# Attention in unrolled half-groups: row maxima from row-tiled pairs, probabilities summed over key tiles on VectorE and GpSimd, and a short product with ones

## What is computed

```python
q, k, v = (n(x) @ Wq), (n(x) @ Wk), (n(x) @ Wv)       # n = layernorm; 16 heads, 2 x 16 wide
q, k = rotary(q), rotary(k)
for w in (0, 1):                                       # each head has two query/key pairs
    s_w = q_w @ k_w.T * scale ; masked causally
    attn_w = softmax(s_w) @ v                          # the same v (32 wide) for both
attn = lowpass_over_time(attn_1 - lambda * attn_2)     # FFT, filter, inverse FFT
attn = rms_normalise(attn, 32 wide) ; out = x + attn @ Wout
```

## Time and profile before

| | us |
|---|---|
| median of three runs | 1475.98 (1471.82 to 1480.4) |
| the profiled execution | 1487.37 |
| its span, first to last instruction | 1485.3 |
| `attention`: first projection to first `rows` matmul | 78.89 to 134.98 |
| `attention`: groups in steady order, to the last copy of `acc` | 166.98 to 1025.6 |
| PE busy, of the span | 82% |
| ACT busy, of the span | 55% |
| DVE busy, of the span | 55% |
| POOL busy, of the span | 36% |
| mean granted clock of TensorE (1.0 is full) | 0.902 |

### The profile page before, as it was taken

One profiled execution on the slowest core, in us unless ns is written; L12 is line 12 of the kernel. 1 busy time (PEld: TensorE's weight loads), 2 busy tenths in 40 slices (PEclk: granted clock), 3 DMA queues, 4 the chain that ended last, 5 costly groups with the idle time before them and its releaser, 6 DMA issues. The chain is left out here.

```text
span 1485.3 us, 20587 instructions
## 1 busy us (share of the span) xinstructions
PE 1224.6 (82%) x6617; PEld 636.3 (43%) x6632; DVE 814.1 (55%) x1518; ACT 821.2 (55%) x1757; POOL 529.8 (36%) x487
## 2 busy tenths in 40 slices
PE   5954789789789889789789788788479999996996
PEld 4722233333333333333333332423257777774453
DVE  5644553563663663563563563731756666653775
ACT  2303587787787787687787789775312222220221
POOL 4434404226226226225326321020015656563111
PEclk9986669999989989889989989979879999998997
DMA  4356530620620630620530620300421121102331
GB/s 140 117 135 103 84 55 22 104 34 36 110 29 36 100 38 37 104 36 35 86 54 36 94 31 15 116 2 15 155 80 57 65 71 68 47 32 98 119 107 42
DMA packets 68972, 102.04 MB, mean 69 GB/s; under 512 B 8065, under 2 KB 34305, under 8 KB 68865
## 3 DMA queue, kind: packets, MB, share of 16 engines
q1 hardware_dynamic: 58368, 71.34, 24.3%
q0 software_dynamic: 5888, 20.97, 3.7%
q10 hardware_dynamic: 4608, 8.39, 1.5%
HBM read 66.74 MB, written 33.95 MB: 68 GB/s over the span
## 5 line engine op out<-in xcount | busy, mean ns | idle before, releaser
L1056 ACT ACTIVATE score<-score,nmax 128x1024 f32<-128x1024 f32 (+7 forms) x512 | 364.8, 713 | 167.0 <-DVE nmax L932 83.0
L1086 ACT ACTIVATE prob<-score 128x1024 f32<-128x1024 f32 (+3 forms) x384 | 298.2, 812 | 46.4 <-PE score L793 29.3
L774 PE MATMUL score<-kst,qst 96*128 96x512 bf16 (+3 forms) x768 | 219.8, 366 | 96.5 <-ACT score L1056 76.0
L935 DVE TENSOR_REDUCE nmax<-score 128x1 f32<-128x640 f32 (+3 forms) x256 | 251.0, 1019 | 86.7 <-PE score L778 82.6
L789 PE MATMUL score<-qst,kst 99*128 99x512 bf16 (+3 forms) x768 | 221.8, 359 | 25.1 <-ACT score L1056 9.7
L932 DVE TENSOR_REDUCE nmax<-score 128x2 f32<-128x256 f32 (+3 forms) x128 | 105.2, 824 | 243.2 <-PE score L778 243.2
L718 PE MATMUL misc<-xnT,wg 128*128 128x512 f32 x256 | 139.7, 645 | 24.3 <-DVE raw L872 16.7
L774 PEld LDWEIGHTS score<-kst,qst 96*128 96x128 bf16 x768 | 63.4, 103 | 223.6 <-ACT score L1056 147.0
L789 PEld LDWEIGHTS score<-qst,kst 99*128 99x128 bf16 x768 | 75.1, 104 | 195.7 <-ACT prob L1086 70.8
L778 PE MATMUL score<-mask_s,identb 128*128 128x128 bf16 x512 | 115.8, 236 | 0.0
L793 PE MATMUL score<-mask_t,identb 128*128 128x128 bf16 x512 | 111.3, 240 | 0.0
(11 more groups left out here) (219 smaller groups left out, 2054.1 us busy)
## 6 DMA issues: line engine op xcount, KB each, us to landing
piece_scratch<-pieces POOLq DMA_DIRECT2D x16, 768.0 KB, 4.1
qst<-piece_scratch SPq DMA_DIRECT2D x48, 256.0 KB, 9.5
kst<-piece_scratch SPq DMA_DIRECT2D x48, 256.0 KB, 18.4
x1in<-in_query SPq DMA_DIRECT2D x16, 256.0 KB, 2.7
v_scratch<-v ACTq DMA_DIRECT2D x16, 256.0 KB, 2.0
vg<-v_scratch SPq DMA_DIRECT2D x8, 512.0 KB, 15.0
att_scratch<-y SPq DMA_DIRECT2D x8, 512.0 KB, 2.7
m_aT<-att_scratch SPq DMA_DIRECT2D x16, 256.0 KB, 2.9
```

The costliest lines, as they stand in the source:

```text
L774: mm = nc.tensor.matmul(score[slot][:, bank, 0:w], qst[0:PIECES, g.slot, pair + k, i * P:(i + 1) * P], kst[0:PIECES, g.slot, pair + k, c0: ...
L935: nc.vector.tensor_reduce(nmax[:, pair, i:i + 1], src[:].rearrange("p a b -> p (a b)")[:, 0:(i + 1) * P], AX.X, ALU.max, negate=True).then ...
L1056: ins = nc.scalar.activation(s, s, ACT.Exp, bias=nmax[:, pair + k, i:i + 1], accum_out=den[:, pair + k, i:i + 1])
L1086: nc.scalar.activation(prob[:, u % NPROB, :, t0:HALF], score[slot][:, :, t0:HALF], ACT.Exp).then_inc(s_exp, 1)
```

## The change

- **Half-groups.** A group is worked on as two sets, one for each query/key pair number, of four heads. There are 16 sets; all of them are written out, there is no loop. Stacks `qst` and `kst` have three slots of four heads.
- **`rows` units give the maximum only.** They use the coarse half of the stack: three products of pieces, 48 rows. Even heads keep those rows at partitions 0 to 47, odd heads at 64 to 111 (`BANDS`, `COARSE`), and the matmuls of an even and an odd head are issued one after the other into two banks. A unit is at most 512 columns wide. There is no exp and no sum on ACT; the bank is free when DVE has taken the maximum. Masks of two heads are added by one matmul.
- **`probs` units** are one head each, in one bank, with the full stack (depth 98 or 112). They subtract the negated maximum alone (two bf16 rows), so the probabilities are not normalised.
- **PSUM**: five banks in a ring (`RING`), two for `acc`, one for `misc`.
- **Sums of probabilities**: a tile holds one key tile for four heads. Tiles 0, 4 and 8 of 12 are bases; the tiles 1, 2, 3, 9, 10 and 11 are added to them by DVE and 5, 6 and 7 by POOL, in fp32. `denominators` multiplies the three bases with a matrix of ones, 32 columns a head, into `misc`; ACT forms 1/sum by Ln and Exp (`norm`).
- **`output`** multiplies `acc` with 1/sum, and for the second set with -lambda too (DVE); `vn` and `scale_v` go.
- **Evacuations**: ACT copies out projections, turns and low pass, which DVE did before.
- **DMAs**: 24 for a set's stacks instead of 12 for a group; the same bytes, each DMA a quarter of the size. The shift rows go by one DMA out and two in, for each half of a set.
- All `rows` units of a set are done ahead, merged pair by pair with the 24 pairs of `probs` units of the set before.

The diff, cut to its core:

```diff
 def rows_units():
     units = []
     for i in range(TB):
-        n = 2 if (i + 1) * P <= HALF else 1
-        units += [(i, a, n) for a in range(0, NP, n)]
+        for c0 in range(0, (i + 1) * P, HALF):
+            width = min(HALF, (i + 1) * P - c0)
+            n = 2 if width <= HALF // 2 else 1
+            for first in range(0, 2, n):
+                for odd in range(2):
+                    units.append((i, c0, width, [2 * x + odd for x in range(first, first + n)]))
     return units
...
+BANDS = ((0, 16, 32, 48, 64, 80), (64, 80, 96, 16, 32, 48))
+COARSE = (slice(0, 3 * D), slice(64, 64 + 3 * D))
+VALUES_LATER, ADD_LATER, DEN_LATER, OUT_LATER, SWAP_LATER, SUMS_LATER, MISC_FREE = 3, 4, 7, 10, 4, 6, 3
+BASES = {0: "dve", 4: "pool", 8: "dve"}
+def schedule():
+    pairs += [("rows", 0, u) for u in range(0, NRU, 2)]
+    for n in range(SETS):
+        mine = [("probs", n, m) for m in range(0, NPU, 2)]
+        ahead = [("rows", n + 1, u) for u in range(0, NRU, 2)] if n + 1 < SETS else []
+        pairs += merge(mine, ahead)
...
-        score = [ctx.enter_context(nc.psum_tensor(f"score{i}", [P, 2, HALF], F32)) for i in range(NSLOT)]
-        acc = ctx.enter_context(nc.psum_tensor("acc", [P, HALF], F32))
+        score = [ctx.enter_context(nc.psum_tensor(f"score{i}", [P, HALF], F32)) for i in range(RING)]
+        acc = [ctx.enter_context(nc.psum_tensor(f"acc{i}", [P, HALF], F32)) for i in range(2)]
...
+            def slot_free(k):
+                if k >= RING:
+                    kind, count = done[k - RING]
+                    pe.wait_ge(s_max if kind == "rows" else s_exp, count)
+            def rows(n, u):
+                for x in range(len(heads)):
+                    for odd in range(2):
+                        c, head = COARSE[odd], RU[u + odd][3][x]
+                        mm = nc.tensor.matmul(banks[odd][:, x], qst[c, n % SLOTS, head, i * P:(i + 1) * P],
+                                              kst[c, n % SLOTS, head, c0:c0 + width], start=(x == 0),
+                                              stop=(x == len(heads) - 1), skip_group_check=True)
+                if diag:
+                    for odd in range(2):
+                        nc.tensor.matmul(banks[odd][:, :, width - P:width], identb[:], mask, start=False, stop=True,
+                                         skip_group_check=True).then_inc(s_unit, 1)
+            def denominators(n, h):
+                for b in bases:
+                    for head in range(GH):
+                        mm = nc.tensor.matmul(misc[head * 2 * D:(head + 1) * 2 * D], ones[:], tile_of(n, b)[:, head],
+                                              start=(b == bases[0]), stop=(b == bases[-1]), skip_group_check=True)
...
-                    ins = nc.scalar.activation(s, s, ACT.Exp, bias=nmax[:, pair + k, i:i + 1],
-                                               accum_out=den[:, pair + k, i:i + 1])
+            def add(n, v):                       # on DVE; the same on POOL
+                total = tile_of(n, b)[:, :, t0:HALF]
+                nc.vector.tensor_tensor(total, total, tile_of(n, v)[:, :, t0:HALF], ALU.add).then_inc(s_add["dve"], 1)
+            def norm(n, h):
+                nc.scalar.activation(rden[:, q % 2], misc[:], ACT.Ln).then_inc(s_mread, 1)
+                nc.scalar.activation(rden[:, q % 2], rden[:, q % 2], ACT.Exp, scale=-1.0).then_inc(s_rden, 1)
...
+            for n in range(SETS):                # SP
+                if n + 2 < SETS:
+                    stack(n + 2)
+                if n + 1 < SETS:
+                    shift_in(n + 1, 0)
+                if n % 2 == 0 and g > 0:
+                    store(g - 1)
+                if n + 1 < SETS:
+                    shift_in(n + 1, 1)
```

More of the change, by code:

```diff
@@ L422, in merge @@
     return out + few[done:]
[L425 to L464, removed]
@@ L480, in attention @@
+    order = {name: k + 1 for k, name in enumerate(uses)}
+    opened = None
+    for e in EVENTS:
+        if e[0] in ("part", "use"):
+            assert opened in (None, e[1]), (opened, e)
+            opened = e[1] if e[0] == "part" else None
+    place = {u: k for k, u in enumerate(UNITS)}
+    seen = {"rows": 0, "probs": 0}
+    done = []
+    for kind, _, _ in UNITS:
+        seen[kind] += 1
+        done.append((kind, seen[kind]))
     with ExitStack() as ctx:
@@ L797, in values @@
-            def values(g, m):
-                h, j, which, _ = PU[m]
-                pe.wait_ge(s_exp, count(g, place_of(g, "probs", m)))
-                t0 = max(j * P - h * HALF, 0)
-                if j == 0 and which == 0:
-                    if g.reg is not None or g.c > 0 or h:
-                        pe.wait_ge(s_oT, g.times(2, h))
-                end = j == (h + 1) * TB // 2 - 1 and which == 1
-                for head in range(GH):
-                    pslot = (m - 1 + head // 2) % NPROB
-                    v = (vg, vn)[which]
-                    mm = nc.tensor.matmul(acc[head * 32:head * 32 + 32, t0:HALF],
-                                          v[:, g.slot, j, head * 32:head * 32 + 32],
-                                          prob[:, pslot, head % 2, t0:HALF],
-                                          start=(j == 0 and which == 0), stop=end, skip_group_check=True)
-                mm.then_inc(s_pv, 1)
@@ L1013, in _ @@
+            g = NG - 1
+            for h in range(2):
+                dve.wait_ge(s_mread, order["low", g, h])
+                if h == 0:
+                    dve.wait_ge(s_att, 2 * g)
+                nc.vector.tensor_tensor(sq[:, half(h)], y[:, half(h)], y[:, half(h)], ALU.mult).then_inc(s_sq, 1)
+            for h in range(2):
+                square(g, h)
+            for h in range(2):
+                ch = Chain(dve, s_newton, Step(None, g, 2), 8)
                 ch.n = 4 * h
-                dve.wait_ge(s_rs, g.times(4, 2 * h + 2))
@@ new lines, in _ @@
+            nc.gpsimd.memset(parity(kst[SHIFT[1]], 1), 1.0).then_inc(s_ones, 1)
+            pool.wait_ge(s_ones, 5)
+            pool.wait_ge(s_const, 16 * 12)
+            for part in range(4):
+                rotate(1, 0, part)
+            for kind, x, u in EVENTS:
+                if kind == "add":
+                    if u in ADDS["pool"]:
+                        add(x, u)
+                elif kind == "rotate":
+                    rotate(*x)
+                elif kind == "squares":
+                    squares(x, u)
+                elif kind == "newton":
+                    for h in range(2):
+                        normalised(x, h)
```

962 lines of the change are left out of this document (488 added, 474 removed).

## The result

The changed kernel takes 1562.76 us (median of 4 runs, 1559.41 to 1566.02) where the kernel before takes 1477.99 (4 runs): 1.059 times the time, with a 95% interval of 1.056 to 1.061. That is 85 us slower; 1388 was forecast, in a range of 1305 to 1465. The time and its sign both missed, and so did the third rival, which had put the slow case at 1517 and given it 0.11.

What follows compares the result with a forecast made beforehand. PE and ACT together were taken to bound `attention`, through three slots waiting for DVE, then ACT. Start 157, sets 750 and last set 30 end at 937 instead of 1025.6: gain 88, median 1388 us, range 1305 to 1465.

Steps and rivals of the forecast that it cites:

- the third rival: In `attention`, coarse pairs don't overlap and every shape change costs its upper price: S above 55.9 us, 1517 us; chance 0.11.
- the 150 of the reading: PE's waits in `attention` before the change, about 150 us of 859, read as mostly for slots ACT had not emptied.
- the steps: PE's work in `attention` at full clock: 596 plus 35 for sets 0 to 14, some 24 for the last.
- (a): In `rows`, whether two 48-row matmuls overlap: full overlap taken, the other end +3.9 us a set.
- (b): On PE, 20 more array shape changes a set, coarse pairs then mask: 0 to 4.6 us, 2.3 taken.
- The 18 us for two sets bound by DVE: In `attention`, two sets without projection or low pass are DVE's: 9 us more each, 18 within the 649.
- 4 us a set, 60: PE's stalls in `attention`, with DVE near 80%, in order, and two pairs of maxima waiting behind every 1.75 us add.
- 7 of rounding up: In the sum for `attention`, 683 plus 60 made 743, taken as 750.
- hidden: POOL's three adds of 2048 elements a set, 14 us, within 33 of about 50 us; cover about one `values` interval.
- S: Time of one set in `attention`: 50 us forecast; the prediction counts as wrong below 46 or above 54.
- The second: Rival with DVE as the bound in `attention`: 42.5 us a set, 80% busy, S = 53, 1432 us; chance 0.19.
- the 0.10 for "slower": Chance that the whole kernel measures above 1483.4 us, given by rival 3; faster had 0.86, same 0.04.

## Why the prediction was wrong, point by point

- **ACT: right in size, wrong in worth.** 548 us after, 530 forecast. But the kernel before did not lose 150 us to ACT alone. It has 118 us of idle PE in its stretch (859 long, 741 busy), not the 150 of the reading, and shortening the exps gave 49.
- **PE's own work: nearly right.** 673 us by the trace, 655 by the steps; both traces show that it did not change (674 before). Overlap (a) is full. (b) was taken at half its upper end, 0.115 us for each of 20 blocks in a set, and is up to 0.21: an estimate from these steps is up to 28 us more in 15 sets, so the 18 can all lie there. No run tests the other terms one by one. The 18 us for two sets bound by DVE stood among PE's work and were divided by the clock with it.
- **DVE's price: in the range as a whole; its effect: the step that failed.** 640 us in the stretch is 40 a set, inside 39 to 42.5. The adds alone took 11.2 a set (178.5 / 16), above the 7.3 to 10.6 forecast. The failed step is the next one: DVE's load was charged at nothing beyond the stalls, "4 us a set, 60", though the prediction says beside it that maxima stand behind every add. In the forecast's stretch of 780 us PE is idle for 91 (60 of stalls, 19 for the sets bound by DVE, 5 in the last set, 7 of rounding up). Measured are 171, 80 more, and without adds 96. Ring and queue explain it: DVE serves PE's banks in order, five banks hold two and a half pairs, and a held add stands for up to 6.6 us before the next maxima.
- **The clock: a consequence that was not carried through.** 673 / 0.86 is 783 us, 673 / 0.95 is 708: 74 more. The forecast tied the clock to no stall. In these runs it goes with them: 0.86 with 171 us idle, 0.90 with 126 (maxima for DVE's adds, POOL's left out), 0.95 with 96 (no adds), 0.98 with 68 (sums on PE).
- **The sum of the miss.** The stretch is 954 - 780 = 174 us longer: 80 idle, 74 by the clock, 19 for 18 us more work at 0.95. It starts 4 us earlier and so ends 170 later. The profiled execution came 167 us above its forecast of 1399; the median 175 above its own, since the profiled one stands 3 us above the median, not 11.
- **POOL's adds: price right, "hidden" wrong.** 4.57 us each, against twice 2.35. Leaving them out gives 35 to 38 us, in part, it seems, through DVE's adds of 1536 (2.6 to 1.8 us).
- **SP: the right queue, too cheap.** 16.8 us instead of 1, 16.2 of it at one place that was not counted: the last shift rows stand behind `weights_ahead`. The prediction does not have the root's wait for POOL, which costs PE 4.6 us in each of seven groups. Orders cost 30 us.
- **The signs that it named.** S was to be at most 54 and is 61; the clock in the steady stretch is above 0.85, just; POOL and shift rows are no releasers of over 30 us for PE itself, though ACT's wait for POOL is 36.
- **The rivals.** The second, DVE as the bound, was nearest in mechanism, but sized by a busy share of 80% (S = 53, 1432 us). DVE costs PE its time at 67%: being held and standing in order count beside its own work. The third gave the right sign and passed its threshold of 55.9 us, but not for its reason: without the row pairs the time is within 7 us. So the 0.10 for "slower" came true by another cause.

What is left open: of the 57 us that unheld work on DVE costs, how much is the lateness of single maxima and how much the clock. No run varies one without the other. Of the 32 us by which the kernel without adds lies above 1388, about 25 are PE's work (679 instead of 655, at 0.95), which no run takes apart.

## What to carry to other kernels

Before work is moved to an engine that others wait for in order, don't ask how full it is: list what stands behind each new operation, how many buffers cover that, and add the resulting idle time's price in clock. Here 116 us of unheld work on a DVE 58% busy cost 57 us, and the same sums as 95 us of extra work on the fullest engine came out 73 us faster than as adds. An elementwise operation with two SBUF inputs, on DVE beside a POOL that reads SBUF, must be priced as its own time plus the rest of what POOL has running, for each such operation, the tiny ones too: here up to 4.8 us on top of 1.75, and 2.0 on top of 0.17.

## What the runs showed of the hardware

- A DVE operation with two SBUF inputs and a POOL operation that reads SBUF exclude each other, whole operation by whole operation: 16 elements took 0.17 to 2.2 us, 1536 elements 1.75 to 6.6, while single-input maxima of the same sizes stayed at their time (677, 1208, 1743 ns), and so did an operation with one input in PSUM (678 to 692).
- The one that waits does not always come next: the add that began at 629.48 let a POOL operation of 630.64 pass, and ran when that was over. Of the 66 operations of DVE that were held for over 0.3 us, 60 ran when the POOL operation then running had ended, six only after one or two that POOL began later.
- Two matmuls of 48 rows and 512 columns in the two halves of the array overlap fully (0.215 us for both); going into this shape from the whole array and out of it again costs 0.21 us, as much as the overlap saves. Beside a `values` block that side costs nothing more.
- Each of 22 waits of PE of 3.1 to 6.4 us was followed by 6 us at a granted clock of 0.50 to 0.74 (0.60 from 452 to 458, after 4.6 us idle), so that a wait costs more than its length.
